# A gated delta-rule solve regrouped: four images in four 32-row groups, sequence halves as planes

## The reference, cut to what matters

```
q, k, v = silu(x @ Wq), l2norm(silu(x @ Wk)), silu(x @ Wv)
log_f = log_sigmoid(x @ Wf)                 # 16 columns, one for each head
gamma = -sigmoid(x @ Wgamma)                # 16 columns, one for each head
a = k * gamma * exp(log_f)
for each token:
    Sp = S * exp(log_f)
    u  = a . Sp + v
    S  = Sp + outer(k, u)
    o  = q . S
```

## Time and profile before

| | |
|---|---|
| median of three runs | 2023.65 us |
| profiled execution, own time | 2023.33 us |
| its span | 2021.3 us |
| mean granted TensorE clock | 0.876 of full |
| TensorE busy with multiplies | 1769.4 us (88%) |
| VectorE / ScalarE / GpSimd busy | 1084.5 / 672.3 / 299.6 us |
| the eleven delta stages | about 1304 to 1850 us of the span |

### The profile page before, as it was taken

The page is one execution under the profiler, slowest core; times in us unless marked ns, Lnnn a source line. Parts: engine busy times, 40 slices in busy tenths (PEclk is TensorE's granted clock), DMA queues, the critical chain, the costliest instruction groups (busy, mean ns, idle before and its releaser), DMA issues. The chain is left out here.

```text
span 2021.3 us, 52149 instructions
## 1 busy us (share of the span) xinstructions
PE 1769.4 (88%) x22817; PEld 1573.1 (78%) x22817; DVE 1084.5 (54%) x2346; ACT 672.3 (33%) x1389; POOL 299.6 (15%) x302
## 2 busy tenths in 40 slices
PE   5677786799999999999999999778999889777589
PEld 4466675579888999999999989566788778767468
DVE  3655555584546545545555455545534454442885
ACT  3344444432223222223223232354333333223133
POOL 0322232610000000000000000332222222100540
PEclk9788898899999999999999999788776877655579
DMA  4100000100001000000000000100000000001001
GB/s 142 50 2 1 0 0 2 65 21 22 22 1 43 1 22 21 22 22 22 22 21 22 1 1 1 34 2 2 3 4 3 3 3 4 4 4 47 1 7 44
DMA packets 9943, 36.03 MB, mean 18 GB/s; under 512 B 3056, under 2 KB 5896, under 8 KB 7176
## 3 DMA queue, kind: packets, MB, share of 16 engines
q1 hardware_dynamic: 9736, 32.96, 4.7%
HBM read 30.47 MB, written 2.49 MB: 16 GB/s over the span
## 5 line engine op out<-in xcount | busy, mean ns | idle before, releaser
L1042 ACT ACTIVATE hidden<-bank,moe_b 128x512 f32<-128x512 f32 (+1 forms) x320 | 213.3, 668 | 537.1 <-PE bank L934 526.1
L951 PE MATMUL bank<-moe_w2h,hidden_hi 128*128 128x256 f32 x1216 | 345.7, 284 | 0.0
L951 PE MATMUL bank<-moe_w2l,hidden_hi 128*128 128x256 f32 x1216 | 344.0, 283 | 0.0
L951 PE MATMUL bank<-moe_w2h,hidden_lo 128*128 128x256 f32 x1216 | 344.0, 283 | 0.0
L934 PE MATMUL bank<-x_hi,moe_w1h 128*128 128x512 f32 (+1 forms) x640 | 243.8, 381 | 2.9 <-ACT hidden L1042 2.8
L934 PE MATMUL bank<-x_lo,moe_w1h 128*128 128x512 f32 (+1 forms) x640 | 242.5, 379 | 0.0
L934 PE MATMUL bank<-x_hi,moe_w1l 128*128 128x512 f32 (+1 forms) x640 | 242.0, 378 | 0.0
L951 PEld LDWEIGHTS bank<-moe_w2h,hidden_hi 128*128 128x128 f32 x1216 | 233.1, 192 | 5.9 <-DVE residual L1076 4.3
L951 PEld LDWEIGHTS bank<-moe_w2l,hidden_hi 128*128 128x128 f32 x1216 | 233.2, 192 | 1.2
L951 PEld LDWEIGHTS bank<-moe_w2h,hidden_lo 128*128 128x128 f32 x1216 | 233.2, 192 | 0.0
L1076 DVE SCALAR_TENSOR_TENSOR residual<-bank,gates,residual 128x256 f32<-128x256 f32 x152 | 73.4, 484 | 290.4 <-PE bank L951 290.4
(11 more groups left out here) (284 smaller groups left out, 3531.5 us busy)
## 6 DMA issues: line engine op xcount, KB each, us to landing
moe_w<-in_moe_w SPq DMA_DIRECT2D x16, 1024.0 KB, 4.8
patches<-in_patches SPq DMA_DIRECT2D x8, 864.0 KB, 4.5
out<-residual SPq DMA_DIRECT2D x19, 128.0 KB, 1.7
ffn_w<-in_ffn_w SPq DMA_DIRECT2D x2, 1024.0 KB, 6.4
att_w<-in_att_w SPq DMA_DIRECT2D x1, 1536.0 KB, 5.9
delta_w<-in_delta_w SPq DMA_DIRECT2D x1, 1280.0 KB
tok_w<-in_tok_w SPq DMA_DIRECT2D x1, 768.0 KB, 4.1
delta_wvf<-in_delta_wvf SPq DMA_DIRECT2D x1, 272.0 KB
```

The lines of the kernel that those rows point to most:

```text
L951: mm = nc.tensor.matmul(bank[4 + n % 3][:, 0:D], left, right, start=(i == 0), stop=(i == len(passes) - 1))
L1042: nc.scalar.activation(H[:, i % 4, 0:n], bank[i % 4][:, 0:n], ACT.Relu, bias=b1[:, x, f:f + 1]).then_inc(acted, 1)
```

## The change

A chunk is now 2 quads of 4 images. Image r of a quad lies in rows 32r to 32r+18, and the two halves of the sequence are two planes in the free dimension. Lanes fall from 64 to 32, and each buffer has the two planes.

- Products with PSUM row group r now use rows 32r of SBUF as well. `first_half`, `remainder` and `second_half` still have 128 products each, but they cycle through four row groups instead of two. `score` handles each image and each half of the keys by itself: 2 x 128 products with 32 weight columns, 76 or 38 moving. `output` has 256 products with 32 rows, 38 or 19 columns moving. `inverse_out` has 76 products with 32 weight columns, 64 moving. `a_rows` has 76.
- GAMMA and F projections of 256 features are gone. Gamma's 16 columns are appended to the values' weights (288 columns), and -gamma x forget (`step_scale`) scales the rows of A as they are taken in (`a_out`) and the rest (`with_values`), not the keys.
- The decay product is in fp32r, with the log-forget split into two parts on VectorE; 4 batches of 456 columns instead of 8 of 304; a second constant matrix (`whole`) adds the plain sum over a half. GpSimd writes 3 tiles of steps per batch.
- u has its own padded buffer, cleared once. `values` now stand ahead of `a_rows`, and two `decay` batches stand between the solves.

```diff
-    jobs = ((K, 0), (K, 1), (Q, 0), (Q, 1), (GAMMA, 0), (F, 0), (GAMMA, 1), (F, 1))
+    jobs = ((K, 0), (K, 1), (Q, 0), (Q, 1))
...
-                nc.tensor.matmul(bank[4 + b % 2][:, 0:CT], identb[:, :], spread(past[:, :], 1, HPH),
-                                 start=True, stop=False)
-                nc.tensor.matmul(bank[4 + b % 2][:, 0:CT], after[:, :],
-                                 MS[:, b % 2].rearrange("p g t -> p (g t)"),
+                to = bank[4 + b % 2]
+                for part in range(2):
+                    nc.tensor.matmul(to[:, 0:BATCH], after[:, :], MS[:, b % 2, part], start=(part == 0), stop=False)
+                for part in range(2):
+                    nc.tensor.matmul(to[:, across], whole[:, :], MS[:, b % 2, part, later], start=False, stop=False)
+                nc.tensor.matmul(to[:, 0:across.start], identb[:, :], spread(past[:, :], 1, 2 * HPH),
                                  start=False, stop=True).then_inc(d_log, 1)
...
                 for m in range(HALVES):
                     for e in range(2):
-                        ts = slice((2 * m + e) * 2 * SEQ, (2 * m + e + 1) * 2 * SEQ)
-                        for s in range(2):
-                            for g in range(PPH):
-                                rows = slice(g * QUAD, (g + 1) * QUAD)
-                                mm = nc.tensor.matmul(psum[half(s), g, ts], KX[rows, m, 2 * p + s, e, :],
-                                                      QA[rows, m, 2 * p + s].rearrange("p x t -> p (x t)"),
-                                                      start=True, stop=True)
+                        for h in range(PLANES):
+                            n = (2 * m + e) * ROW
+                            ts = slice(n + 2 * SEQ, n + ROW) if h else slice(n, n + 2 * SEQ)
+                            for r in range(4):
+                                for g in range(PPH):
+                                    of = rows(g)
+                                    mm = nc.tensor.matmul(
+                                        psum[rows(r), g, ts], KX[of, m, 4 * q + r, e, h * HB:(h + 1) * HB],
+                                        QKc[of, m, 4 * q + r, :, h * HALF:SEQ], start=True, stop=True)
...
                 for i, t in enumerate(T_BATCHES[k]):
-                    for s in range(2):
-                        mm = nc.tensor.matmul(psum[half(s), 6 + k % 2, i * LANES:(i + 1) * LANES],
-                                              TT[half(s)].rearrange("p h c t -> p (h c) t")[:, :, t],
-                                              ident[half(s), half(s)], start=True, stop=True)
+                    for r in range(4):
+                        of = half(r % 2)
+                        mm = nc.tensor.matmul(psum[rows(r), 6 + k % 2, i * PAD:(i + 1) * PAD],
+                                              TT[of, r // 2, :, t], ident[of, of], start=True, stop=True)
...
+                for m in range(HALVES):
+                    for q in range(QUADS):
+                        n = (m * QUADS + q) * SEQ
+                        for h in range(PLANES):
+                            ts = slice(n + HALF, n + SEQ) if h else slice(n, n + SEQ)
+                            qs = slice(2 * SEQ, 2 * SEQ + HALF) if h else slice(0, SEQ)
+                            for e in range(2):
+                                for r in range(4):
+                                    for g in range(PPH):
+                                        lane = q * HEADS + m * HPH + 2 * g + e
+                                        mm = nc.tensor.matmul(
+                                            bank[r][rows(g), ts], UB[rows(r), lane, h, :],
+                                            PA[rows(r), y % 2, lane, qs],
+                                            start=(h == 0 and e == 0), stop=(h == 1 and e == 1))
...
+            for q in range(QUADS):
+                for h in range(PLANES):
+                    values(q, h)
+            low_part(0)
+            low_part(1)
             a_rows()
-            for p in range(IP):
-                values(p)
-            low_part(0)
+            project(0)
+            project(1)
+            low_part(2)
             first_half(0)
             first_half(1)
-            project(0)
-            low_part(1)
-            remainder(0)
-            project(1)
-            low_part(2)
-            remainder(1)
             project(2)
             low_part(3)
-            second_half(0)
+            remainder(0)
             project(3)
             low_part(4)
+            remainder(1)
+            decay(0)
+            second_half(0)
+            decay(1)
             second_half(1)
-            project(4)
-            project(5)
-            output()
-            project(6)
-            project(7)
             key_norm(0)
             key_norm(1)
-            decay(0)
-            decay(1)
+            output()
+            decay(2)
+            decay(3)
             score(0)
             inverse_out(0)
-            decay(2)
             inverse_out(1)
-            decay(3)
             score(1)
             inverse_out(2)
...
+                nc.gpsimd.tensor_tensor(
+                    MS[:, b % 2, :, later].rearrange("p n (g t) -> p n g t", t=HALF),
+                    spread(LF[:, :, 1, q, heads].bitcast(F32), 3, HALF),
+                    spread(spread(here[:, 0:HALF], 1, HPH), 1, 2), ALU.mult).then_inc(steps_ready, 1)
+                for part in range(2):
+                    nc.gpsimd.tensor_tensor(
+                        MS[:, b % 2, part, later.stop:BATCH].rearrange("p (n g t) -> p n g t", n=2, t=HALF),
+                        spread(spread(LF[:, part, 0, q, heads].bitcast(F32), 2, HALF), 1, 2),
+                        spread(here[:, :].rearrange("p (n t) -> p n t", n=2), 2, HPH),
+                        ALU.mult).then_inc(steps_ready, 1)
```

More of the change, by code:

```diff
@@ L1241, in norm_into_output @@
                                         ALU.add).then_inc(scaled, 1)
[L1243 to L1246, removed]
+            blocks = [(slice(HB * r, HB * r + HALF), slice(0, HALF)) for r in range(4)]
+            blocks += [(slice(HB * r + HALF, HB * (r + 1)), slice(SEQ, SEQ + HB - HALF)) for r in range(4)]
             def zero_gate(done):
@@ L1379, in delta_buffers @@
     return {
[L1380 to L1385, removed]
+        "PA": sb(ctx, "qk_and_ak", [P, 2, LANES, ROW]),
+        "VH": sb(ctx, "values", [P, 3, PLANES, QUADS, D]),
@@ L1399, in delta_buffers @@
     }
 def delta_stage(nc, psum, bank, buffers, c, nxt, z, y):
[L1407 to L1412, removed]
+    Q, K, O = range(3)
@@ new lines, in delta_stage @@
+    (PA, VH, SH, SL, KQ, SQ, KX, SV, GZ, UB, RX, LF, PD, LZ, MS, DS, AS, TT, TS) = (buffers[n] for n in (
+        "PA", "VH", "SH", "SL", "KQ", "SQ", "KX", "SV", "GZ", "UB", "RX", "LF", "PD", "LZ", "MS", "DS", "AS", "TT",
+        "TS"))
+    (wh, wl, wvfh, wvfl, same, after, whole, past, here, emask, ident, identb, XH, XL, xh_c, xl_c) = (
+        buffers[n] for n in ("wh", "wl", "wvfh", "wvfl", "same", "after", "whole", "past", "here", "emask", "ident",
+                             "identb", "XH", "XL", "xh_c", "xl_c"))
@@ L1422, in delta_stage, with rows @@
[L1422 to L1427, removed]
+    jobs = ((K, 0), (K, 1), (Q, 0), (Q, 1))
+    first_cols, later_cols = slice(0, HPH * SEQ), slice(HPH * SEQ, BATCH)
+    later, across = slice(0, HPH * HALF), slice(HPH * SEQ, BATCH)
+    def rows(r):
+        return slice(r * HB, (r + 1) * HB)
@@ L1576, in first_half @@
                 if z is not None:
-                    pe.wait_ge(a_taken, 2)
-                for lane in range(LANES)[lanes(j)]:
-                    for s in range(2):
-                        rows = block_rows(2 * s)
-                        mm = nc.tensor.matmul(psum[rows, j, place(lane)],
-                                              TS[rows, lane * HALF:lane * HALF + HB], vh_y[rows, lane, :],
-                                              start=True, stop=True)
+                    pe.wait_ge(a_taken, 1)
@@ L1595, in remainder, with second_half @@
                                               start=True, stop=True)
                 mm.then_inc(r_done, 1)
-            def second_half(j):
+            def second_half(q):
                 if y is None:
                     return
-                pe.wait_ge(rx_ready, j + 1)
-                for lane in range(LANES)[lanes(j)]:
-                    for s in range(2):
-                        rows = block_rows(2 * s + 1)
-                        mm = nc.tensor.matmul(psum[rows, j, place(lane)],
-                                              TS[rows, lane * HALF:lane * HALF + HB], RX[rows, lane, :],
-                                              start=True, stop=True)
+                pe.wait_ge(rx_ready, q + 1)
+                for g in range(HEADS):
+                    lane = q * HEADS + g
+                    for r in range(4):
```

(7 more changed lines are left out.)

493 lines of the change are left out of this document (238 added, 255 removed).

## The result

The changed kernel takes 2097.03 us (four runs, 2091.61 to 2097.32) beside 2024.59 for the kernel before on the same chip: ratio 1.0349, 95% interval 1.0329 to 1.0369, slower by 72.4 us. The forecast was 2072 us, 49 more. Direction and mechanism were right, the size was a third short.

A forecast was written before the change was run, and what follows sets the result against it. TensorE's instruction blocks, at least 3.47 us per 256 instructions, were taken as the bound. Full stages (69.0 us for 64.1) gave +24.5, partial stages +11.6, +12, +5.6 and -3.5: +50, taken as 49, so 2072 us, range 2030 to 2105.

The forecast's parts named there:

- The reading of the profile: TensorE's list sets the pace: each block of 256 instructions takes at least 3.47 us, and one block may be ahead.
- Rival 1: Stops are not a price of each block; dense pairs go at 13 ns, so faster: 1988 us, chance 0.13.
- rival 2: Small tiles get in each other's way; a full stage takes 77 us, the program 2124 us, chance 0.12.
- rival 3: Everything hides behind the blocks and savings cancel them: 63 us a full stage, 2020 to 2033 us, chance 0.05.
- the signs of being wrong: Outputs' 512 multiplies under 7 us, two blocks closer than 3.4 us, or stage end set by VectorE's inverse rows.
- the block's 3.47 us: Least time for 256 TensorE instructions, 27.1 ns a load and multiply pair; 2168 pairs a full stage make 17 blocks, 59 us.
- values, A's rows, two projections: Start of a full stage: values 5.0 us, A's rows 5.3, two projections at the half clock spacing 3.0.
- first solves to second score: Middle of a full stage: first solves 5.5 us, outputs 12.1, first score 5.6, inverse_out 5.3, second score 5.4, among others.
- end of stage: Weigh of two batches, then 0.88 us to the next stage: 3.75 us with the start-up.
- The partial stages: Stages outside the five full ones: k = 8 +11.6 us, k = 9 and 10 +6 each, k = 2 0, k = 0 -3.5.
- k = 1: Nothing to solve; GpSimd becomes the chain, then two dense scores with a weigh after each: 35.6 us for 30.0, +5.6.
- The savings: In a full stage, 24 projections x 0.25 = 6.0 us and the fewer decays 1.9 us.

The follow-up runs named there:

- gates alone: Kernel before with 256-wide gate projections dropped, gate as 16 columns beside the values, groups, halves and decays as before: 2006.97 us, ratio 0.9921.
- gates and decays: Kernel before with 16-column gates and decays as two fp32r products from split logs, groups, halves and 64-row scores as before: 2016.84 us, ratio 0.9968.
- regrouped, second-half products left out: Kernel after without the products of the second sequence half in scores and outputs, 4096 pairs fewer: 1980.79 us, ratio 0.9792.
- the streams: Separate kernel that stores zeros and runs TensorE alone through six product streams, s_a to s_f; short products restart 3.46, 3.73 or 4.00 us apart.
- the missing pairs: Kernel after without second-half products in scores and outputs, 1980.79 us, and without those of the scores alone, 2039.20 us.
- the narrow products: Kernel after with only 4 columns of each score and output product moved: 2087.52 us, ratio 1.0319.
- s_d: Fourth stream of the TensorE-only kernel: 1024 bf16 products of 32x32 over 38 columns; restarts 3.46, 3.73 or 4.00 us apart.

## Why the prediction was right, and where it was short

Five steps from before to after, by the medians:

| kernel | us | step |
|---|---|---|
| before | 2024.4 | |
| gates alone | 2007.0 | -17.4 |
| gates and decays | 2016.8 | +9.9 |
| regrouped, second-half products left out | 1980.8 | -36.0 |
| + second-half products of the outputs, 2048 pairs | 2039.2 | +58.4 |
| + those of the scores, 2048 pairs = after | 2097.0 | +57.8 |

The third kernel to the fourth changes more than one thing, and the fourth computes less; the step says only that regrouping saves when it adds no pairs.

*The reading of the profile* held. 256 instructions a block (the streams' 12544 loads and multiplies came in 49 packets), 128 multiplies between restarts, one block ahead, 17 packets in k = 5 (16 or 17 forecast), 2168 multiplies, VectorE 29.5 us busy for 28.9 and ScalarE 18.9 for 22.2. Rival 1 is refuted by the streams and by the missing pairs, rival 2 as the main cause by the narrow products, rival 3 by the time itself: 72.2 us a full stage for its 63. Of the signs of being wrong, one restart in k = 8 came 3.30 us after the one before, under the 3.4 named; no full stage ended on VectorE's inverse rows, and the outputs took 12.9 us. The fetch of instructions isn't hidden for products this small: 126 us of waits and the 116 us that went with 4096 pairs say so. The packets of the instruction queue that end 1.19 to 1.60 us ahead of each of 45 restarts (35 in the streams, 10 in k = 5) show that it is the fetch.

*The term that was mis-sized is the block's 3.47 us.* That was the smallest distance of restarts, seen twice. In the delta stages of the kernel after 15 distances between restarts are near it, 31 near 3.75 and 21 near 4.02; the mean of a block is 3.63 to 3.67 us, and 3.85 in k = 10. Stage k = 5 by the forecast's parts:

| part | forecast | measured |
|---|---|---|
| values, A's rows, two projections | 13.3 | 12.0 |
| first solves to second score (15.3 blocks) | 51.9 | 56.2 |
| end of stage | 3.75 | 3.7 |

The middle was forecast at 3.39 us a block, since it took some blocks as ahead at the outputs and scores; in a stretch of fifteen only one is. Inside it errors cancelled: the first solves took 3.5 us for 5.5, with no stop, and the remainders, outputs and scores behind them paid for it. That is +3.2 us in each full stage by the mean (72.2 for 69.0), 16 of the 23 us missed.

*The partial stages:* k = 8 +15.9 us (forecast +11.6, the same cause), k = 9 +6.4 and k = 10 +7.3 (+6 each), k = 2 +1.8 (0), k = 0 and the part ahead -3.2 (-3.5). Behind the delta stages the program is 1.8 us shorter, for which the forecast has no term.

*k = 1 was +7.2 for +5.6, but the step failed, and the near number is luck.* The forecast made GpSimd's steps the chain. Without the 256 score pairs the stage takes 29.8 us, as before the change, and GpSimd's waits (0.83 and 1.63 us ahead of the first decays) stand in both kernels. It is two blocks again.

*The savings* were too high in the prediction's text, though the sum didn't rest on them: 24 projections were 5.1 us, not 6.0, as half of them ran at full clock, and most of it comes back. The two fp32r decays for one were counted as a gain of 1.9 us a stage; on before's groups they cost 0.9 in a full stage, and in the kernel after decays stand in a dense stretch where even longer ones are free.

*Open:* why a block takes 3.46, 3.73 or 4.00 us and not one time. The streams show the same three without the kernel's traffic. The packets take different times, 0.88 to 1.45 us in the streams; whether that makes the steps is not shown.

The fastest version that computes everything is the one with the gates alone, 2006.97 us and ratio 0.9921 (0.9902 to 0.9940), less than 1% under the kernel before.

## What to carry to other kernels

Count TensorE's instructions before its columns: where products were short, a load and multiply pair cost about 28 ns (28.4 and 28.2 by the pairs left out; 27 to 31 in the streams, at 4 columns as at 38), so a layout that doubles the pairs has to save that much elsewhere. Less work in a product is no cure: nine tenths fewer columns gave 9.5 us, half of the pairs in scores and outputs 116. Wider weights, as the kernel before has them, need fewer pairs; the regrouped layout was not run with them. To recognise such a stretch, look for waits on nothing, 128 multiplies between stops, and one packet of the instruction queue in each. Price a block by the mean of a long dense stretch, not by the shortest distance, and count only one as ahead. In such a stretch long products are free: adding 48 cost nothing. Removing 24 a stage from the kernel before gave 1.8 us of their 5.1, and moving them uncovered the waits they hid.

## What the hardware showed that was not expected

The distance of restarts comes in steps of 0.27 us (3.46, 3.73, 4.00). Inside a burst, pairs of 32x32 tiles start 8 to 13 ns apart (128 in 1.23 to 1.90 us), pairs of 128x128 tiles 25 ns apart, so with 32x32 tiles TensorE stands still for 1.5 to 2.8 us of each 3.46 to 4.00. TensorE's granted clock was lower where there were more stops: 0.76, 0.66 and 0.57 in the full stages shown of the kernel before, the gates alone and the kernel after, and 0.50 in k = 9 and 10, where nothing but bursts is left (before the change too). The profile of the streams has no record of the clock and prints 1.00, but behind s_d the first products of 512 columns start 427 ns apart and the later ones, without stops, 216 ns: 1.20 and 2.37 columns a nanosecond, which are the 1.2 and 2.4 GHz of the streams' expectation, and the 0.25 and 0.13 us for 304 columns of the earlier trace rows.
